# Attention and a feed-forward block on one core: the second batch's queries in groups of 256, with 3.5 first-pass units a step, and edits at the start, the scales and the last tiles

## The reference

```python
x = L0_attn_x                                   # (2, 1024, 512)
qk = (x @ Wqk_w.T + Wqk_b).reshape(b, n, H, E, 2)     # H = 8, E = 8
v = (x @ Wv_w.T + Wv_b).reshape(b, n, H, E)
scores = jnp.einsum('bhqd,bhkd->bhqk', q, k)
attn = jax.nn.softmax(scores, axis=-1) / HEAD_DIM ** 0.5
x = _layernorm(x + (attn @ v) @ Wo_w.T + Wo_b)
...
gate = silu(x @ Wg.T); up = x @ Wu.T            # 1792 wide, weights dequantized in groups of 128
x = _layernorm(x + (gate * up) @ Wd.T)
```

## Time and profile before

| what | value |
|---|---|
| time, median of 3 runs | 521.45 us (521.42 to 521.49) |
| time of the profiled execution | 521.81 us |
| its span, first to last instruction | 519.7 us |
| granted TensorE clock | 0.998 of full speed |
| PE, DVE, ACT, POOL busy | 501.1, 413.0, 405.5, 255.7 us |
| instructions | 8086 |

### The profile page before, as it was taken

The page is one execution under the profiler, slowest core; times in us unless marked ns, Lnnn a source line. Parts: engine busy times, 40 slices in busy tenths (PEclk is TensorE's granted clock), DMA queues, the critical chain, the costliest instruction groups (busy, mean ns, idle before and its releaser), DMA issues.

```text
span 519.7 us, 8086 instructions
## 1 busy us (share of the span) xinstructions
PE 501.1 (96%) x2976; PEld 193.2 (37%) x2976; DVE 413.0 (79%) x705; ACT 405.5 (78%) x558; POOL 255.7 (49%) x295
## 2 busy tenths in 40 slices
PE   8899999999999999999999999999999999999994
PEld 3222222323222322234444444444444444444441
DVE  3699999989999997368878778778668666788677
ACT  1522888998899989877888888888888888888880
POOL 9100091823100715073464676664997962648741
PEclk9999999999999999999999999999999999999999
DMA  6410018576530005700031121140020020000022
GB/s 192 136 68 5 21 35 211 182 144 125 91 59 1 3 5 103 276 7 1 1 59 24 20 43 21 20 62 1 1 81 1 0 83 0 3 0 1 0 81 81
DMA packets 30151, 29.20 MB, mean 56 GB/s; under 512 B 19489, under 2 KB 21921, under 8 KB 29857
## 3 DMA queue, kind: packets, MB, share of 16 engines
q1 hardware_dynamic: 26688, 22.67, 15.7%
q0 software_dynamic: 3424, 6.03, 6.3%
HBM read 24.37 MB, written 4.23 MB: 55 GB/s over the span
## 4 chain that ended last, share of the span: by engine, by line
PE 79%; DVE 7%; POOL 5%; ACT 5%; issue 2%; DMA 1%; SPq 0%; DVEq 0%; POOLq 0%; ACTq 0%
PE ps L1123 16%; PE ps L1135 16%; PE ps L1157 16%; PE ps L1068 9%; PE ps L1039 6%; PE ps L963 6%; DVE mxh L1249 4%; ACT pbuf L760 3%; PE ps L892 3%; POOL x L617 2%; PE ps L1051 1%; PE ps L902 1%; PE ps L1016 1%; POOL stack L663 1%; DMA arena<-xT 1%
## 5 line engine op out<-in xcount | busy, mean ns | idle before, releaser
L1249 DVE TENSOR_REDUCE mxh<-ps 128x1 f32<-128x512 f32 x256 | 157.0, 680 | 6.5 <-PE ps L963 5.3
L760 ACT ACTIVATE pbuf<-ps,gamma 128x1024 f32<-128x1024 f32 x128 | 140.5, 1114 | 16.2 <-PE ps L1039 11.2
L841 ACT ACTIVATE ps<-ps,ratio 128x512 f32<-128x512 f32 x168 | 106.5, 659 | 40.4 <-PE ps L1123 37.3
L1157 PE MATMUL ps<-wd,stack 128*128 128x512 f16 x440 | 129.7, 379 | 0.7 <-POOL stack L663 0.6
L1123 PE MATMUL ps<-arena,wg 128*128 128x512 f16 x448 | 115.5, 379 | 0.1
L1135 PE MATMUL ps<-arena,wu 128*128 128x512 f16 x448 | 115.3, 379 | 0.1
L1423 DVE TENSOR_TENSOR ps<-ps,stack 128x512 f32<-128x512 f32 x128 | 87.8, 695 | 33.4 <-PE ps L1157 31.7
L847 ACT ACTIVATE ps<-ps,ratio 128x512 f32<-128x512 f32 x156 | 98.9, 659 | 6.6 <-PE ps L1135 2.3
L661 POOL CAST stack<-pbuf 128x512 f16<-128x512 f32 x55 | 33.5, 609 | 76.5 <-DVE pbuf L1398 76.5
L1423 DVE TENSOR_TENSOR ps<-ps,pbuf 128x512 f32<-128x512 f32 x76 | 52.6, 695 | 23.2 <-PE ps L1157 22.5
L1068 PE MATMUL ps<-pbuf,arena 128*32 128x256 f32 x832 | 66.5, 391 | 1.7 <-ACT avt L767 1.7
(11 more groups left out here) (120 smaller groups left out, 387.4 us busy)
## 6 DMA issues: line engine op xcount, KB each, us to landing
arena<-xT SPq DMA_DIRECT2D x16, 256.0 KB, 5.8
x<-x SPq DMA_DIRECT2D x2, 2048.0 KB, 10.0
out<-x SPq DMA_DIRECT2D x3, 1024.0 KB, 4.2
stack<-down_ratios SPq DMA_DIRECT2D x1, 2048.0 KB, 9.6
wg<-gq POOLq DMA_DIRECT2D x4, 448.0 KB, 7.3
wu<-uq POOLq DMA_DIRECT2D x4, 448.0 KB, 7.4
wd<-dq POOLq DMA_DIRECT2D x2, 896.0 KB, 10.3
pbuf<-down_ratios SPq DMA_DIRECT2D x1, 1536.0 KB, 6.2
```

The costliest lines, as they stand in the source:

```text
L760: nc.scalar.activation(pbuf[:, pi % 4, :].rearrange("p (a n) -> p a n", a=2), ps[:, at:at + 2, :], ACT.Exp, scale=gamma[:, n // (ALL // B) ...
L841: nc.scalar.activation(gbank[t % 2], gbank[t % 2], ACT.Copy, scale=gr[:, t % G, c:c + 1])\
L1157: mm = nc.tensor.matmul(bank[k], mparts[:, a, t % NM, k * P:(k + 1) * P], wd[:, i, :], start=(i == 0 and a == 0), stop=(a == 1), skip_grou ...
L1249: nc.vector.tensor_reduce(mxh[:, f % 2, qh, half:half + 1], ring_bank("first", n), AX.X, ALU.max)\
```

## The change

It has these parts.

- Blocks 2 and 3 are worked in groups `f` of 256 queries: `GROUPS` has four wide groups (the turns of blocks 0 and 1) and eight narrow ones of 16 units and four steps each. A step of a narrow group takes 256 keys of 256 queries, so `scores` has four matmuls of 256 columns a pair, and one half of `av` takes the first 128 keys, the other the next. There are still 64 steps and 256 units. `M` turns come in the steps 29, 33, 37, 41, 45, 49, 53 and 57 from there on, and `av_out` of 256 columns every four steps.
- From step 24 (`SLOWER`) on, the pairs get 2, 1, 2 and 2 units, 3.5 a step, so that the units end in step 56.
- `DRAIN` is step 57, and the projections of blocks 1 and 2 stand in six steps in a row. `av` is in halves there too.
- `max_rows` has four transfers of three rows in place of two, for wide groups too.
- VectorE's statistics of block 0 stand between the reductions (steps 38, 43, 46, 51), with two reciprocals and the mean and variance (48, 52); GpSimd takes over the other operations of the ratios, and its addition of the output bias to batch 1 is cut into four.
- At the start a matmul with one row adds the bias of q and k in PSUM, after six idle matmuls in place of ten; the largest magnitudes, the high and the low part are taken from PSUM; four small matmuls turn the magnitudes so that each partition has them, and `cast_scales` and `place_scales` go, for both batches. VectorE keeps the first q rows. Half of the clearing of `arena` goes to GpSimd.
- `scale_residual` runs in the periods 26, 27, 33 to 35 and 40 to 44. Of the last four tiles ScalarE normalises three, with a shift that GpSimd makes.

The core of the diff:

```diff
+WIDE = [(u, g, 0, BT) for u in range(NB // 2) for g in range(NG)]
+NARROW = [(u, g, q, BT // 2) for u in range(NB // 2, NB) for g in range(NG) for q in (0, BT // 2)]
+GROUPS = WIDE + NARROW
+NF = len(GROUPS)
+TURNS = NB * NG
+UNIT0 = [sum(2 * HG * group[3] for group in GROUPS[:f]) for f in range(NF + 1)]
+STEP0 = [sum(2 * group[3] for group in GROUPS[:f]) for f in range(NF + 1)]
+FG = UNIT0[1]
+FIRST = UNIT0[NF]
 AHEAD = FG + 14
+SLOWER = STEP0[3]
 TILES = NB * G
 LAG = 3
...
+        def issued_before(n, pair):
+            return min(AHEAD + 4 * n + 2 * pair - max(0, n - SLOWER + 1) // 2, FIRST)
+
...
-            m = AHEAD + 4 * n + 2 * pair
-            return range(m, min(m + 2, FIRST))
+            return range(issued_before(n, pair), issued_before(n + pair, 1 - pair))
...
-        LASTF = NB * NG - 2
-        DRAIN = ALL - 11
-        ASIDE = {DRAIN: ("attT", 1, 0), DRAIN + 1: ("wo", 1, 0), DRAIN + 3: ("wo", 1, 1), DRAIN + 4: ("avT", LASTF, 0),
-                 DRAIN + 6: ("attT", 2, 0), DRAIN + 7: ("wo", 2, 0), DRAIN + 9: ("wo", 2, 1)}
+        STATS0_AT = (38, 43, 46, 51)
+        AVT_AT = (9, 17, 25, 34, 42, 50, 58)
+        LAST_OF_TURN = [max(f for f in range(NF) if GROUPS[f][:2] == (a // NG, a % NG)) for a in range(TURNS)]
+        DRAIN = ALL - 7
+        ASIDE = {DRAIN: ("attT", 1, 0), DRAIN + 1: ("wo", 1, 0), DRAIN + 2: ("wo", 1, 1), DRAIN + 3: ("attT", 2, 0),
+                 DRAIN + 4: ("wo", 2, 0), DRAIN + 5: ("wo", 2, 1)}
...
-        RESIDUAL_AT = 28
+        RESIDUAL_AT = (26, 27, 33, 34, 35, 40, 41, 42, 43, 44)
...
-                for jj in range(2):
-                    r = ROWS * jj + MROW
-                    sp.dma_start(qs[b][r:r + 3, k, 2 * g:2 * g + 2, :],
-                                 mrows[6 * BT * jj:6 * BT * (jj + 1), f % 2, :]).then_inc(s_mld[g], 16)
+                for c in range(HG):
+                    r, t = ROWS * (c // 2) + MROW, 2 * g + c % 2
+                    sp.dma_start(qs[b][r:r + 3, k, t, q * P:(q + count) * P],
+                                 mrows[3 * count * c:3 * count * (c + 1), f % 2, :]).then_inc(s_mld[f % 4], 16)
...
+                if 5 <= f < 9:
+                    add_bias(N // P + 2 * (f - 5), 2)
+                if f in (2, 3, 4, 5):
+                    load_weights(f)
+                if f == 8:
+                    guard_down_scales()
+                if f == 9:
+                    scale_ratios()
+                if f == 10:
+                    down_ratios()
...
             def av_out(f):
-                act.wait_ge(s_av, 2 * (f + 1) * KT)
-                if f >= 2:
-                    act.wait_ge(s_of, turn_count["avT", f - 2, 0])
-                nc.scalar.activation(avt[:, f % 2, :], bank[AVB], ACT.Copy).then_inc(s_ave, 1)
+                act.wait_ge(s_av, 2 * STEP0[f + 1])
+                u, g, q, count = GROUPS[f]
+                a, own = NG * u + g, slice(q * P, (q + count) * P)
...
+            for i, k in enumerate(LAST_ORDER[:BY_ACT]):
+                act.wait_ge(s_bn, BT * (2 * NB - 1) + i + 1)
+                act.wait_ge(s_shift, i // 2 + 1)
+                nc.scalar.activation(x1[:, (NB - 1) * BT + k, :], bank[k], ACT.Identity, bias=shift[:, k:k + 1],
+                                     scale=rstd[:, k:k + 1]).then_inc(s_resa, 1)
...
                 return [(qk, k, c) for k in range(2) for c in range(C)] + [(v, 0), (v, 1), (turn_tops, 0, bank[3]), (v, 2),
-                                                                           (cast_scales, 0, bank[3]), (v, 3), (vt,)]
+                                                                           (v, 3), (vt,)]

             def turn_tops(b, dst):
                 pe.wait_ge(s_topc, b + 1)
                 if b == 0:
                     pe.wait_ge(s_id, 2)
-                nc.tensor.transpose(dst[0:1, 0:P], tops[:, 2:3], ident[:]).then_inc(s_rf if b else s_turned, 1)
-
-            def cast_scales(b, dst):
-                pe.wait_ge(s_row, 5 * (b + 1))
-                if b == 0:
-                    pe.wait_ge(s_pick, 1)
-                nc.tensor.matmul(dst[:, P:P + 3], onerow[:], row[0:1, 4:7], start=True, stop=True)\
-                  .then_inc(s_rf if b else s_cast, 1)
+                for own in range(2):
+                    for kind in range(2):
+                        at = HD * (kind != own)
+                        mm = nc.tensor.matmul(dst[own * HD:(own + 1) * HD, at:at + HD], tops[:, 2:3].to_broadcast([P, HD]),
+                                              ident[:, kind * HD:(kind + 1) * HD], start=True, stop=True)
+                mm.then_inc(s_rf if b else s_turned, 1)
...
+                for i in range(BT // count):
+                    kt = BT // count * (n - STEP0[f]) + i
+                    for j in range(2):
+                        rows, t = slice(ROWS * j, ROWS * (j + 1)), 2 * g + pair
+                        mm = nc.tensor.matmul(bank[at + j][:, i * own:(i + 1) * own], ks[b][rows, t, kt * P:(kt + 1) * P],
+                                              qs[b][rows, k, t, q * P:(q + count) * P], start=True, stop=True)
                 mm.then_inc(s_scf, 1)
...
+                if step == 0 and n:
+                    pe.wait_ge(s_ave, f)
+                lo, width = half * TB // 2, TB // 2
+                if count == BT:
+                    kt, to = step, lo
+                    first = step == 0 and half == 0
+                else:
+                    kt, to = 2 * step + half, q * P
+                    first = kt == 0
                 for j in range(HG):
-                    mm = nc.tensor.matmul(bank[AVB][j * VC:(j + 1) * VC, lo:hi], vst[b][:, kt, g * HG + j, :],
-                                          pbuf[:, (2 * n + j // 2) % 4, (j % 2) * TB + lo:(j % 2) * TB + hi],
-                                          start=(kt == 0 and half == 0), stop=(kt == KT - 1), skip_group_check=True)
...
-            for _ in range(10):
+            for _ in range(6):
                 nc.tensor.matmul(bank[7], still[:, 0:P], still[:], start=True, stop=True)
+            pe.wait_ge(s_brow, 16)
+            pe.wait_ge(s_ones, 1)
+            for k in range(2):
+                nc.tensor.matmul(bank[k], brow[:], ones[:], start=True, stop=False, skip_group_check=True)
...
+                if b:
+                    dve.wait_ge(s_projr, (2, 4)[k])
+                    src = qkf[:, k * TB:(k + 1) * TB]
+                else:
+                    dve.wait_ge(s_proj, k + 1)
+                    src = bank[k]
+                nc.vector.tensor_reduce(tops[:, k:k + 1], src, AX.X, ALU.max, apply_absolute_value=True).then_inc(s_top, 1)
...
+                    nc.vector.scalar_tensor_tensor(out=low[:, cols], in0=bank[k], scalar=unit[:, 0:1],
                                                    in1=high[:, cols], op0=ALU.mult, op1=ALU.subtract).then_inc(s_low, 1)

+            def keep_first_q():
+
+                dve.wait_ge(s_put, 2)
+                nc.vector.tensor_copy(qs[0][:, 0, 0, :], put_bank(1)).then_inc(s_kept1, 1)
...
-            for k in range(BT):
-                attention_stats(0, k)
-            mean_variance(0)
+                if n in STATS0_AT:
+                    attention_stats(0, STATS0_AT.index(n))
+                if n == 48:
+                    invert_scales()
+                if n == 52:
+                    invert_down_scales()
+                    mean_variance(0)
             att_out(1)
-            down_ratios()
+            apply(0, range(2))
+            normalise(TURNS - 2)
             for t in range(2):
                 add_output(1, t)
-            apply(0)
-            scale_ratios()
+            apply(0, range(2, BT))
             for t in range(2, BT):
                 add_output(1, t)
-            normalise(LASTF)
             att_out(2)
             for t in range(BT):
                 add_output(2, t)
```

374 lines of the change are left out of this document (188 added, 186 removed).

## The result

| | median | runs | profiled execution: time, span |
|---|---|---|---|
| before | 521.43 us (521.18 to 521.49) | 4 | 521.81, 519.7 |
| changed | 526.81 us (526.31 to 527.32) | 4 | 527.32, 524.9 |

The change makes the kernel slower: the ratio is 1.0104, with a 95% interval from 1.0087 to 1.0122. The forecast was 520.0.

The account below looks back on a forecast made before the run. VectorE was taken as the bound up to step 52, TensorE only 0.17 us a step behind. Gains 0.8 + 0.4 + 0.6 + 0.1 + 2.0 less 2.5 made 1.4, from 521.45 to 520.0 us; range 516.0 to 523.2.

Parts of the forecast that it names:

- the bias matmul and the magnitudes from PSUM take away one pass: Start: one ScalarE pass of 0.69 us goes, but it lies under the v matmuls, so it gains nothing.
- The forecast's steps to the high part: Start: from the row's reduction at 15.62 to the high part at 16.85 instead of 17.56 us, gaining 0.7.
- the gain of 2.0: Steps 24 to 56 at 3.5 units a step: 81.7 us against 83.7 before.
- seven turns of maxima: Steps 29 to 53: each bank swap makes the next score wait for an exponential, 0.4 us each, 2.8 in all.
- `av_out`, two wide and six narrow: Steps 24 to 56: wide copies delay ScalarE 0.3 us each, narrow ones cost 0.05 each, 0.9 in all.
- VectorE's new work: Steps 24 to 56: statistics, reciprocals, mean and variance take 4.2 us between reductions, 0.8 of it on the path.
- narrow scores: Steps 24 to 56: two rounds of 256 columns with new weights cost 0.4 us in all for 50 pairs.
- the step rate doesn't move: Rival, steps 24 to 56: 3.5 units only shift VectorE's idle time, gain 0 instead of 2.0, time 522.0 us; chance 0.14.
- VectorE alone is the bound: Rival, steps 24 to 56: turns and loop cost nothing beyond VectorE's reductions, 76 us, time 514.3; chance 0.20, including halfway.
- Steps 57 to 63: End of attention: crowded turns and waits, 0.9 us at the second `wo`, make 17.6 us against 15.1, 2.5 lost.
- the last tiles: Kernel's end: four VectorE passes of 0.72 us become three on ScalarE beside one, gaining 0.1 us.
- Maxima landing late: Rival, turns of maxima: four transfers land at 4.4 us, scores need them at 4.35; up to 3 us lost, 523.0; chance 0.07.

Follow-up runs that it names:

- the loads later: GpSimd's two last down-weight issues moved one group later, against the changed kernel with 128-row bias matmuls and four units a step: 525.83 us.
- the early drain: Block 1 and 2 turns begin at step 53 over eleven steps, against the narrow, four-unit, 128-row-bias kernel with down weights issued later: 523.68 us.
- wide run: Changed kernel with 128-row bias matmuls, but the old attention: all groups wide, four units a step, block 1 and 2 turns from step 53; 521.05 us.

## Why the prediction was wrong

The path from the kernel before to the changed one goes edit by edit. The second column has the differences of medians, the third those of the traces from the first exponential to the last instruction, in which the scatter of the start has no part:

| step of the path | medians, us | traces, us |
|---|---|---|
| start, scales, feed-forward part, last tiles, sixth `avT` in the shared banks (wide) | -0.74 | +0.46 |
| narrow groups (and the loads later) | +1.04 | +0.81 |
| statistics and reciprocals inside the loop | +1.68 | +1.91 |
| turns of blocks 1 and 2 in seven steps instead of eleven | +2.15 | +2.00 |
| 3.5 units a step (and the loads earlier) | -1.78 | -2.31 |
| bias matmuls of one row instead of 128 | +3.03 | +0.02 |
| sum | +5.38 | +2.89 |

Of the 5.2 us of span, the other 2.3 are the start: 3.0 later by the clock, 0.7 earlier by the rest.

**The start: failed.** The step was "the bias matmul and the magnitudes from PSUM take away one pass ... nothing there", and the sum 0.8 gained. The bias matmuls themselves, and the six idle ones in place of ten, have no price in it at all. Six idle matmuls and four one-row passes in place of ten idle matmuls were not looked at as what brings the clock up. They delayed the higher level from 5.77 to 11.81 us, and changing only their height gave 3.0 us back. The rest of the start was about right: in the nine profiled executions with full-height bias the first exponential stands at 50.24 to 51.47, 0.4 to 1.7 us earlier than the 51.89 of before. (The forecast's steps to the high part, 0.28, four of 0.19 and 0.35 late, add up to 17.01 and not to 16.85. After the change the way from that reduction at 18.98 to the high part at 19.91 takes 0.93 us, where it took 1.94, so the gain of 0.7 was about right all the same.)

**Steps 24 to 56: the gain of 2.0 was a loss of 0.5.** The pure steps were right. Mis-sized were the terms added to them. Read off the lengths of the single steps, over a pure step of 2.27:

| term | forecast | measured |
|---|---|---|
| 33 pure steps | 74.9 | 74.9 |
| seven turns of maxima | 2.8 | 4.0 |
| four `avT` | 1.9 | 2.3 |
| `av_out`, two wide and six narrow | 0.9 | 2.0 |
| VectorE's new work | 0.8 | 1.1 |
| narrow scores | 0.4 | 0 |
| sum | 81.7 | 84.3 |

Step 53, 3.17 us long, counts with 0.6 as a turn and with 0.3 as new work, since a first-pass unit there waits for a reduction behind a reciprocal and the mean and variance. A turn of maxima costs 0.6 in a narrow group (2.87 against 2.28), forecast 0.4; the one turn at a wide group costs 0.44, and no run separates why. A narrow copy of the `av` bank was to cost 0.05, "since ScalarE has 0.2 a step free". ScalarE isn't what counts there: TensorE has one bank for `av`, and the next group can't begin in it before the copy (2.3 us of waits for L846 on the page); the steps with such a copy behind them (36 and 40 for example) are 2.47 long, 0.2 over a pure one. Over eight steps nothing moved, since narrow groups put twice as many turns and copies on the path as the 3.5 units took off it.

Of the rivals "the step rate doesn't move" (gain 0 in this stretch) came nearest. What the 3.5 units bought is room for VectorE's new work: with them it costs some 1.1 us by the single steps, at four units 1.7 to 1.9. "VectorE alone is the bound" is excluded: VectorE is idle 5 us more, and the steps are no shorter.

**Steps 57 to 63: right in mechanism, 0.9 short.** Forecast 17.6, measured 18.46. The long wait for the second `wo` is there. The turn of maxima (forecast 0.2) waits 0.88 for an exponential. Of the 3.4 us by which the stretch got longer, 1.9 are the price of units that end in step 56, since going back to the early drain takes them off steps 57 to 62: the banks that the turns need come free four steps later. The other 1.5 stay with the early drain (steps 57 and 58, 2.73 and 3.19 us): they are the turn of maxima and the `avT` that narrow groups have so late.

**The smaller terms: right but for the last tiles.** Scales of the second batch: forecast 0.4, measured 0.56. The wait of the down matmul is gone (0.0 in the page's row of L1245), and TensorE reaches its final eight matmuls (L1151 before, L1239 now) 1.0 us sooner after the end of attention, where 0.6 was forecast. But from the end of attention to the last instruction the trace is only 0.44 shorter where 0.7 was forecast, because the last tiles lose 0.5 instead of gaining 0.1. Their normalisation is as forecast in the timeline of ScalarE after: two, and a third that waits for its shift, 0.26 us; VectorE does the fourth beside them, from 520.31 to 521.12.

```profile
519.26 1.45 ACT L963 ACTIVATE x<-ps,shift,rstd 128x512 f32<-128x512 f32 x2 [7.62 <-POOL shift L778]
...
520.97 0.78 ACT L963 ACTIVATE x<-ps,shift,rstd 128x512 f32<-128x512 f32 x1 [0.26 <-POOL shift L778]
```

What follows isn't. SyncE issues the tiles in a fixed order, so that VectorE's finished tile is issued last, at 522.15, behind the third of ScalarE (521.77):

```profile
520.07 2.52 SPq L534 DMA_DIRECT2D out<-x  x4
```

From the first of those final matmuls to the end of the four issues it is 8.58 us (514.00 to 522.59), before 8.23 (509.38 to 517.61), and the last transfer lands another 0.2 later. In the wide runs it lands 0.6 to 0.9 later still, and no run shows why.

**Narrow scores: right.** TensorE in the timeline after, one narrow pair:

```profile
155.02 0.11 PEld L1127 LDWEIGHTS ps<-stack 64*128 64x128 f16 x4 [0.41 <-issue]
155.02 0.39 PE L1127 MATMUL ps<-stack 64*128 64x256 f16 x4
155.25 0.38 PE L1048 MATMUL ps<-stack 64*128 64x512 f16 x2
```

The first unit starts 0.23 us after the score, as it did behind a wide score, and the second round of the score starts 0.12 after the first. All four weight loads are over 0.11 us after the first has begun. So those of the second round are hidden, though they go to the same row groups, against the Trainium skill's rule that the prediction weighed ("TensorE: Matmul & The Clock Gate", Part 3). The same part also says that a load into the background weight buffer is pulled ahead of matmuls in flight, and that fits. Maxima landing late was no cause either: the four transfers are issued in 2.9 us (204.10 to 207.01 in the last turn), and in steps 24 to 56 the waits of TensorE for a transfer of maxima come to 0.4 us, once.

**Open.** What in TensorE's activity the chip counts for its clock is not settled: the runs show that height matters behind six idle matmuls, not how. The sixth `avT` is worth 0.4 us by medians and 0.6 by the step; the medians' scatter doesn't tell them apart. Narrow groups alone cost 0.67 in steps 24 to 56 and 0.85 in steps 57 to 63 by the traces, less 0.7 after attention, where the last transfer of the wide run lands late. Wide groups with 3.5 units, and the changed kernel with its statistics behind the loop, were not run.

## What to carry to other kernels

- At the start of a kernel, price every matmul also by what it does to the clock. A matmul that uses one row is a poor one to stand before the clock has risen; filled up with zeros to full height it costs the same passes and gave 3 us back here.
- Where two limits stand 0.17 us a step apart, relieving one brings little, and anything that comes with the relief (more turns, more copies out of a single bank, work that ends later) is paid in full. Count such pieces per group before making groups smaller.
- Take a difference of a microsecond from traces, stretch by stretch, where the start scatters by as much.
- If a resource is freed four steps later, ask what was planned into those four steps.

## What the runs showed of the hardware

- One-row matmuls do not bring the granted clock up as full-height ones do: behind six idle matmuls the higher level is recorded from 11.81 against 6.34 us, with the same number of matmuls at the same place.
- Amid full-height matmuls at the higher level, a one-row matmul of two passes costs some 1.15 us (1.58 from the start of the pass before it to the start of the pass behind it), where two full-height passes take 0.86.
- VectorE's addition of 128x8 numbers in SBUF took 2.00 us beside a GpSimd addition in SBUF, and 0.17 alone. Two such collisions, through what waited for them, and the drop of the clock that came with them cost 3.9 us in steps 24 to 56.
- The start of identical code scatters: the higher level is recorded from 4.0 to 7.0 us in the executions with full-height bias, and first exponentials lie 1.2 us apart.
